# Flamingo block on one core: another queue order and opening for the first attention, another passage to the second, last weights split in 16 pieces

## The reference

```python
x = x + jnp.tanh(g_xattn[0]) * _L0_xattn_ref(_layernorm(x), ctx, fside, fside, Wq, Wkv, Wout, bout)
x = x + jnp.tanh(g_ffn[0])   * _L0_ffn_ref(_layernorm(x), router, gate_up, down, sh_gate, sh_up, sh_down, shared_gate)
x = x + jnp.tanh(g_xattn[1]) * _L1_xattn_ref(_layernorm(x), ctx, mask, Wq, Wk, Wv, Wo)
x = x + jnp.tanh(g_ffn[1])   * _L1_ffn_ref(x=_layernorm(x), Wg1, Wg2, Wup, bup, Wdown, bdown)
```

## Time and profile before

| | us |
|---|---|
| runs | 1830.37, 1835.76, 1840.65; median 1835.76 |
| the profiled execution, its own time | 1849.24 |
| its span (first to last instruction) | 1847.3 |
| PE busy | 1627.3 (88%) |
| VectorE (DVE) busy | 1158.1 (63%) |
| ACT busy | 733.5 (40%) |
| POOL busy | 411.9 (22%) |

### The profile page before, as it was taken

How to read it: one execution, slowest core, us unless ns; L and a number is a source line. 1 busy time by engine, 2 the same in 40 slices (tenths; PEclk the granted TensorE clock), 3 DMA queues, 4 the chain that set the end, 5 groups by cost and what they waited for, 6 DMA issues and landing times.

```text
span 1847.3 us, 42322 instructions
## 1 busy us (share of the span) xinstructions
PE 1627.3 (88%) x14740; PEld 1365.1 (74%) x14740; DVE 1158.1 (63%) x2986; ACT 733.5 (40%) x1494; POOL 411.9 (22%) x448
## 2 busy tenths in 40 slices
PE   2888988887798999999679999999999998699998
PEld 1555655555576778999678888888888887487887
DVE  4677777776566565555566666666666664465655
ACT  1555555553223223555333333333333332234443
POOL 2555555540323221000111212111121200000000
PEclk9899999999899999999889999999999998799999
DMA  7466566561101002543300000000000000000000
GB/s 190 100 118 117 117 117 117 117 115 33 46 31 39 23 27 79 175 128 114 126 21 21 20 28 20 26 20 26 20 23 26 23 11 7 5 12 23 11 23 23
DMA packets 127355, 107.06 MB, mean 58 GB/s; under 512 B 10442, under 2 KB 120195, under 8 KB 127020
## 3 DMA queue, kind: packets, MB, share of 16 engines
q1 hardware_dynamic: 121068, 89.07, 19.9%
q0 software_dynamic: 6208, 16.95, 2.9%
HBM read 49.22 MB, written 56.77 MB: 57 GB/s over the span
## 4 chain that ended last, share of the span: by engine, by line
PE 50%; DVE 24%; issue 12%; ACT 6%; DMA 3%; SPq 2%; DVEq 2%; another core or an unknown queue 1%; ACTq 0%; POOL 0%; POOLq 0%
PE bank L531 11%; PE bank L532 10%; PE bank L533 9%; PE bank L1006 3%; PE bank L602 2%; PE bank L1034 2%; PE bank L593 2%; DVE probs_b L2253 2%; DVE rm_b L2250 2%; PE bank L557 2%; DVE probs_a L1701 1%; DVE x L2154 1%; DVE oT_b_lo L2242 1%; PE bank L616 1%
## 5 line engine op out<-in xcount | busy, mean ns | idle before, releaser
L1567 POOL TENSOR_TENSOR probs_b<-probs_b,rs_b 128x512 f32<-128x512 f32 x64 | 66.7, 1043 | 483.1 <-DVE rs_b L2263 482.8
L531 PE MATMUL bank<-xT_b_hi,m_hi 128*128 128x256 f32 x512 | 153.7, 300 | 20.1 <-ACT qT L1376 12.0
L1397 ACT ACTIVATE probs_b<-probs_b 128x512 f32<-128x512 f32 x64 | 40.4, 632 | 324.1 <-DVE probs_b L2253 324.1
L531 PE MATMUL bank<-n_hi,oT_b_hi 128*128 128x256 f32 x512 | 149.8, 293 | 5.7 <-DVE x L2221 5.7
L532 PE MATMUL bank<-xT_b_hi,m_lo 128*128 128x256 f32 x512 | 145.7, 285 | 0.0
L533 PE MATMUL bank<-xT_b_lo,m_hi 128*128 128x256 f32 x512 | 145.6, 284 | 0.0
L532 PE MATMUL bank<-n_hi,oT_b_lo 128*128 128x256 f32 x512 | 145.2, 284 | 0.0
L533 PE MATMUL bank<-n_lo,oT_b_hi 128*128 128x256 f32 x512 | 145.1, 283 | 0.0
L1180 ACT ACTIVATE probs_a<-probs_a 128x512 f32<-128x512 f32 x128 | 80.3, 627 | 135.8 <-DVE probs_a L1701 135.2
L1006 PEld LDWEIGHTS bank<-ctxT_b,qT 128*128 128x128 f32 x1024 | 126.3, 194 | 2.7
L1006 PE MATMUL bank<-ctxT_b,qT 128*128 128x64 f32 x1024 | 122.7, 274 | 0.0
(11 more groups left out here) (316 smaller groups left out, 4919.3 us busy)
## 6 DMA issues: line engine op xcount, KB each, us to landing
sorted_x<-zeros SPq DMA_DIRECT2D x16, 2112.0 KB, 13.9
xg<-sorted_x SPq DMA_DIRECT2D x71, 128.0 KB, 2.1
sorted_y<-ys SPq DMA_DIRECT2D x71, 128.0 KB, 1.9
w_raw<-in_w SPq DMA_DIRECT2D x16, 408.0 KB, 4.0
x<-in_x SPq DMA_DIRECT2D x4, 1024.0 KB, 8.9
cx_raw<-in_ctx SPq DMA_DIRECT2D x32, 128.0 KB
out<-x SPq DMA_DIRECT2D x8, 512.0 KB, 2.9
ctxT_a<-in_ctxT SPq DMA_DIRECT2D x16, 128.0 KB, 2.1
```

The lines of the kernel that those rows point to most:

```text
L531: pe.matmul(dst, lh, rh, start=start, stop=False, skip_group_check=True)
L1567: pool.tensor_tensor(probs_b[b], probs_b[b], rs_b[:, b, :].unsqueeze(2).broadcast_to([P, G1, S]), ALU.mult).then_inc(s["b_probs"], 1)
```

## The change

- SP: only the first piece of `x` is loaded ahead of the tables; wv gets a semaphore of its own; pieces 1 to 3 of `x` come after wv; the rest of the tables is loaded in round 0, after the values of round 0.
- VectorE: statistics of piece 0 (8 tiles), 1/sd by integer guess and three Newton steps (`rsqrt`, L1640 on, in place of the root on ACT), keys(0), statistics of piece 1, queries(0), round 0. Pieces 2 and 3 are done inside round 0, the router weights are split after it. `queries(i+1)` moves from p = 1 to p = 2, ahead of `weigh0`.
- PE: transpose of x, both halves of the queries and values one slot later. ACT: `xT_copy` and `v_keep` one slot later. POOL: `queries_in` two slots later, the weights' low half one slot later; in the opening the masked keys before the queries.
- Passage: `w1_raw` is loaded after the first context of attention 1, so PE's `n` waits for `o1_raw` alone; VectorE does n_lo(0), tiles 0 and 1, n_lo(1), n_lo(2), statistics and norm, the other n_lo; PE's `turn_x1(0)` no longer waits for n_lo and `ones`. Tile 3 and the statistics of round 1 go into round 0, after `centre(0)`.
- `w1` is split in 16 pieces of 128x256, one in each round of the second attention: high half on ACT between `oth(i, 1)` and `pth(i, 2)`, low half on POOL at the round's end. The split on VectorE is gone.

```diff
             load_x(0)
-            load_x(1)
...
-                load_x(2 + n)
...
+            for n in range(1, 4):
+                load_x(n)
...
-            load_tables(slice(EARLY, NT * S), "tables_rest")
...
-            with sp.Fori(0, NA - 1) as i:
+            def next_round(i, rest=False):
                 sp.wait_ge(s["a_v_psum"], START + 1 + i)
                 load_context(i + 1)
+                if rest:
+                    load_tables(slice(EARLY, NT * S), "tables_rest")
                 load_round(i)
...
-            sp.dma_start(w1_raw, a["w1"]).then_inc(s["o1_loaded"], 16)
...
+            load_round1(0)
+            sp.dma_start(w1_raw, a["w1"]).then_inc(s["o1_loaded"], 16)
+            with sp.Fori(1, NA) as i:
+                load_round1(i)
...
                         if t == 0:
                             keys(i + 1)
-                        if t == 1:
+                        if t == 2:
                             turn_x(i + 1)
-                        if t in (2, 3):
-                            queries(i + 1, t - 2)
-                        if t == 5:
+                        if t in (3, 4):
+                            queries(i + 1, t - 3)
+                        if t == 6:
                             values(i + 1)
...
-            pe.wait_ge(s["o1_loaded"], 32)
+            pe.wait_ge(s["o1_loaded"], 16)
...
-            pe.wait_ge(s["mask_ready"], 2)
-            pe.wait_ge(s["n_copied"], H1 // 2)
-            pe.wait_ge(s["mask_ready"], 3)
...
             turn_x1(0, first=True)
+            pe.wait_ge(s["n_copied"], H1 // 2)
             for c in range(H1 // 2):
                 queries1(0, c)
+            pe.wait_ge(s["mask_ready"], 3)
...
                 oth(i, 1)
+                act.wait_ge(s["o1_loaded"], 32)
+                act.activation(w1_hi[:, ds(i * W1S, W1S)], w1_raw[:, ds(i * W1S, W1S)], ACT.Copy).then_inc(s["w0_hi"], 1)
                 pth(i, 2)
...
-                    if n == 4 and not last:
+                    if n == 6 and not last:
                         queries_in(i + 1, 0)
-                    if n == 5 and not last:
+                    if n == 7 and not last:
                         queries_in(i + 1, 1)
-                    if n == 6:
+                    if n == 7:
...
+                if first:
+                    pool.wait_ge(s["tables_rest"], 64)
...
+                pool.wait_ge(s["w0_hi"], START + NA + i + 1)
+                pool.tensor_tensor(w1_lo[:, i * W1S:i * W1S + W1S], w1_raw[:, i * W1S:i * W1S + W1S],
+                                   w1_hi[:, i * W1S:i * W1S + W1S], ALU.subtract).then_inc(s["w1_split"], 1)
...
-            stats(0)
+            def moments_x(n, at):
+
+                ve.wait_ge(s[f"x{n}_loaded"], 16)
+                for t in range(8):
+                    st.done(ve.bn_stats(bn[:, t, :], x[:, 8 * n + t, :]))
+                st.wait()
+                for t in range(8):
+                    st.done(ve.bn_aggr(mv_new[:, at + t, :], bn[:, t, :]))
+                st.wait()
+
+            moments_x(0, 0)
+            rsqrt(rstd[:, 0:8], nmr[:, 0:8], 8, 8)
             ve.sem_inc(s["stats_ready"], 1)
...
+                    if p == 2 and not last:
+                        queries(i + 1)
+                    if first and p < 2:
+                        moments_x(2 + p, 8 * p)
+                    if first and p == 1:
+                        rsqrt(rstd[:, 16:32], nmr[:, 16:32], 8, 16)
                     if p >= 2:
                         weigh0(i, p - 2)
...
-                    if p == 1 and not last:
-                        queries(i + 1)
...
             keys(0)
+            moments_x(1, 0)
+            rsqrt(rstd[:, 8:16], nmr[:, 8:16], 8, 8)
             queries(0)
-            ve.wait_ge(s["sel0_loaded"], 16)
+            attend0(0, first=True)
+            ve.wait_ge(s["w0x_loaded"], 160)
             st.done(ve.tensor_copy(rw0_hi, rw0_raw))
...
             ve.wait_ge(s["tables_rest"], 64)
-            attend0(0, first=True)
...
-            add_tile(0, more=1)
-            add_tile(1, yg1)
-            stats_b(0)
-            norm1(0)
             for c in range(H1 // 2):
...
+                if c == 0:
+                    add_tile(0, more=1)
+                    add_tile(1, yg1)
+                if c == 2:
+                    stats_b(0)
+                    norm1(0)
...
                 centre(0)
-                if not first:
+                if first:
+                    add_tile(3)
+                    stats_b(1)
+                else:
                     otl(i - 1, 3)
...
             add_tile(2)
-            add_tile(3)
-            stats_b(1)
-            ve.wait_ge(s["o1_loaded"], 32)
-            st.done(ve.tensor_copy(w1_hi, w1_raw))
-            st.wait()
-            ve.tensor_tensor(w1_lo, w1_raw, w1_hi, ALU.subtract).then_inc(s["w1_split"], 1)
```

More of the change, by code:

```diff
@@ L155, in build @@
         mv = keep.take("mean_var", NT, 2)
-        mv_new = keep.take("mean_var_new", 2 * FT, 2)
-        sd = keep.take("sd", NT)
+        mv_new = keep.take("mean_var_new", 4 * FT, 2)
+        sd = keep.take("sd", 56)
         rstd = keep.take("rstd", NT)
@@ L435, in load_round @@
                     "(p r c) -> p r c", p=P, c=CLEAR), zeros.unsqueeze(1).broadcast_to([P, REPEAT, CLEAR])).then_inc(s["rows_cleared"], 16)
-            with sp.Fori(0, NA - 1) as i:
+            def next_round(i, rest=False):
                 sp.wait_ge(s["a_v_psum"], START + 1 + i)
                 load_context(i + 1)
+                if rest:
+                    load_tables(slice(EARLY, NT * S), "tables_rest")
                 load_round(i)
+            next_round(0, rest=True)
+            with sp.Fori(1, NA - 1) as i:
+                next_round(i)
             load_round(NA - 1)
@@ L499, in _, with load_round1 @@
             sp.wait_ge(s["biases_stored"], 16)
-            with sp.Fori(0, NA) as i:
+            def load_round1(i):
                 sp.wait_ge(s["b_scores"], START + i * 4)
@@ L622, in outputs0, with project0 @@
                 m.then_inc(s["a_o_psum"], 1)
-            def project0(i, n):
+            def project0(i, n, first=False):
                 if n % 2 == 0:
@@ L630, in project0 @@
                     pe.wait_ge(s["a_resid"], START + i * 2 + p // 2)
+                if first and p == 0:
+                    pe.wait_ge(s["w0x_loaded"], 160)
                 m = pe.matmul(bank[5][:, 0:D], oT_a[:, p, :], wo0[:, p % 2, :], start=(p % 2 == 0), stop=(p % 2 == 1))
@@ L635, in late @@
             def late(i, t, lag, step, first):
-                if t >= lag:
+                if t >= lag and first and step is project0:
+                    step(i, t - lag, True)
+                elif t >= lag:
                     step(i, t - lag)
@@ L678, in _ @@
             queries(0, 1)
-            pe.wait_ge(s["w0x_loaded"], 208)
+            pe.wait_ge(s["wv_loaded"], 64)
             values(0)
@@ L1115, in root @@
                 act.wait_ge(s["sd_wanted"], n + 1)
-                act.activation(sd, sd, ACT.Sqrt).then_inc(s["sd_ready"], 1)
-            root(0)
+                act.activation(sd[:, 0:NT], sd[:, 0:NT], ACT.Sqrt).then_inc(s["sd_ready"], 1)
             NS = 8
@@ L1170, in attend0 @@
                 for t in range(NS + 5 if last else NS):
-                    if t == 6 and not last:
+                    if t == 7 and not last:
                         v_keep(i + 1)
@@ L1432, in _ @@
             oth(NA - 1, 3)
-            root(1)
+            root(0)
             ffn("f1", f1, NC1, HID1, False)
@@ L1515, in _ @@
             keys_in(0)
+            for n in range(AHEAD):
+                heads(0, n, first=True)
             queries_in(0, 0, first=True)
             queries_in(0, 1, first=True)
-            for n in range(AHEAD):
-                heads(0, n, first=True)
             bias(0)
-            pool.wait_ge(s["tables_rest"], 64)
             rounds(pool, NA, attend0)
@@ L1601, in _ @@
             ve.tensor_scalar(gbout, gbout, gates[:, 0:1], None, ALU.mult).then_inc(s["gbout_ready"], 1)
-            for n in range(4):
-                ve.wait_ge(s[f"x{n}_loaded"], 16)
-                for t in range(8 * n, 8 * n + 8):
-                    st.done(ve.bn_stats(bn[:, t % 8, :], x[:, t, :]))
-                st.wait()
-                for t in range(8 * n, 8 * n + 8):
-                    st.done(ve.bn_aggr(mv[:, t, :], bn[:, t % 8, :]))
-                st.wait()
             def moments(tile, count):
@@ L1625, in stats @@
             def stats(n):
-                ve.tensor_scalar(sd, mv[:, :, 1], LN_EPS, None, ALU.add).then_inc(s["sd_wanted"], 1)
+                ve.tensor_scalar(sd[:, 0:NT], mv[:, :, 1], LN_EPS, None, ALU.add).then_inc(s["sd_wanted"], 1)
                 ve.wait_ge(s["sd_ready"], n + 1)
-                st.done(ve.reciprocal(rstd, sd))
+                st.done(ve.reciprocal(rstd, sd[:, 0:NT]))
                 st.wait()
@@ L2321, in _ @@
             st.wait()
-            stats(1)
```

(1 more changed line is left out.)

15 lines of the change are left out of this document (8 added, 7 removed).

## The result

The kernel after takes 1815.13 us (median of 4 runs, 1813.28 to 1817.79), the kernel before beside it 1836.08 (4 runs, 1830.37 to 1840.65): ratio 0.9888, 95% interval 0.9861 to 0.9915, 21 us faster. The forecast was 1820. Measured again beside more runs of before the ratio was 0.9881 (0.986 to 0.9902). The kernel before took 1836 us here and 1850 to 1852 us beside the later kernels, so times are compared with those taken beside them, and otherwise only ratios are.

What follows compares the result with a forecast made beforehand. It took loads to bind the opening, a loop of engine hand-overs the first attention's rounds, weight loads and splits the passage, and PE the second attention. 7.2 + 2.1 + 6.4 = 15.7 us off 1835.8 gave 1820, range 1805 to 1834.

Steps and rivals of the forecast that it cites:

- Its sign: Whole kernel: faster, below 1826.6 us, with chance 0.76; same 0.18; slower, above 1844.9 us, 0.06.
- likeliest case: Whole kernel: the forecast itself, 1820 us, by itself 1811 to 1829; chance 0.57.
- Opening, forecast 7.2: Start of kernel: round 1 starts at 64.6 in place of 71.85, gaining 7.2 us, between 4 and 10.5.
- Rounds, forecast 2.1: First attention: a round falls from 23.57 to 23.4 us; 14 rounds x 0.15 = 2.1 us gained.
- The exchange at the centre of the count: First attention round: PE's queries come 2.41 us later, against VectorE's third pair of scores, 2.39 us, moved ahead of the rotary pair.
- a dip of the clock there costs as before: First attention rounds: two chains tie at 23.4 and 23.3 us, so a clock dip costs the same as before.
- Rival B: First attention: VectorE's wait was the bound, the loop falls towards PE's 20.78 us, 20 us more gained, 1800; chance 0.15.
- Passage, forecast 6.4: Passage to second attention: first queries 5.8 us earlier, second maximum at 926.3 against 932.66; 6.4 us gained, between 4 and 9.
- Pieces, forecast 0: Second attention: splitting the last weights in 16 pieces on ACT and POOL costs 0, at most 2 us on ACT.
- Rival D: First attention: PE drops to half clock in every round, 36 us slower, 1856; chance 0.08.

Runs made afterwards that it cites:

- b2_opening: Kernel after with PE, ACT and POOL rounds ordered as before, queries(0) ahead of piece 1's statistics, and one root for pieces 1 to 3: ratio to before 0.9761.
- r_all: Kernel before with only the new order of the first attention's rounds, on PE, ACT, POOL and VectorE: ratio 0.9935, 12 us faster.
- o_open: Kernel before with only the new opening; rounds, passage and last weights as before: ratio 0.996, 7 us faster.
- p_all: Kernel before with only the new passage and the last weights in 16 pieces; opening and first attention as before: ratio 0.995, 9 us faster.
- r_dve: Kernel before with one edit, VectorE's queries(i+1) at p = 2 ahead of weigh0; PE, ACT and POOL as before: ratio 0.9802, 37 us faster.
- b4_norder: b3_tile3 with VectorE's passage order as in before (tiles 0 and 1, statistics and norm ahead of all low halves): 1802.27 us, ratio to before 0.9738.
- b3_tile3: b2_opening with tile 3 and round 1's statistics put back ahead of the second attention's first maximum: 1801.42 us, ratio to before 0.9739.
- r_pe: Kernel before with only the new round order of PE, ACT and POOL; VectorE's queries(i+1) stay at p = 1: ratio 1.0324, 60 us slower.
- w4_pool: Kernel after with each of POOL's 16 subtractions for the last weights done four times: 1827.54 us against 1827.57 for the unchanged kernel after.

## Why the prediction was right, and where its sum was not

Its sign and its likeliest case hold, and 1815.13 is 5 us below 1820. The shares of the three parts don't: the rounds, which it gave least, gave most.

*Opening, forecast 7.2.* Found 6.2 in the profile (with the doubt on the clock of round 0 above), 7 by time. Every mark was 0.5 to 1.1 us late: the shuffle of the queries forecast for 30.6 came at 31.15, round 0 for 35.5 at 36.51, round 1 for 64.6 at 65.68. What it took for granted, that all statistics of piece 1 stand ahead of the first queries, was itself the cost that b2_opening took away.

*Rounds, forecast 2.1.* This is the term that was mis-sized: it measured 9.5 us from the start of round 1 to that of round 15, and r_all is 12 us faster by time. The exchange at the centre of the count is real, but it isn't even. The rotary pair starts 2.23 us later in the round (14.70 against 12.47), not 2.41; behind it VectorE's list is 2.73 us shorter (8.37 against 11.10), not 2.39 + 0.16. That makes 0.50 us a round in place of 0.15, or 13 times 0.50 = 6.4. The second miss was "a dip of the clock there costs as before": the three rounds at a clock of 0.93 are gone, which is another 4.3, and round 1 gives back 1.2 (25.18 against 23.99). Why the falls of the clock went away wasn't tested. But the three profiles with the old rounds (before, o_open, p_all) have two or three of them each, with stops of PE of 1.8 us in every round, and the kernels with shorter stops (1.3 us in after and r_all, 0.7 in r_dve, but for one in round 1) have none. Rival B, the wait as bound, was wrong for this change and right for one half of it: VectorE's move alone gives 21.68. The prediction had both halves' prices, 2.39 and 2.41, and netted them; the step it did not take was to ask whether the second was needed for the first.

*Passage, forecast 6.4.* Found 6.7: 7.1 up to the first queries (forecast 5.8) and -0.4 behind them (forecast 0.6). The new passage was well counted, 25.6 us from the first fold to the queries against a mean of 25.5; what was low is the old one, whose 31.38 is the least of five (mean 32.6). Of the 7.1, 3.5 come from VectorE's order, as b4_norder shows by taking it away, and the rest, by subtraction, from the fold that no longer waits for the other weights. Behind the queries two things cancel. Taking the split of 6.72 us off VectorE is worth 4.5 to 4.8 where tile 3 keeps its place (58.7 against 54.22 and 53.88 in b3_tile3 and b4_norder), and moving tile 3 behind the first maximum costs the 5 that b3_tile3 regains.

*Pieces, forecast 0.* Found 0, with four times the POOL work too.

*Rival D* didn't come: the clock in the rounds is 1.00. Its mechanism is real all the same: r_pe, the same order of PE, ACT and POOL without VectorE's move, runs at 0.88 in its longest rounds, and a round costs 4.4 us more than before, of which the longer wait explains 2.2. The Trainium skill (TensorE: Matmul & The Clock Gate, HAM oscillation) says that the clock falls after idle stretches; the trace of r_pe agrees with it, with one stop of 3.56 us and one fall in each round.

## What to carry to other kernels

When an edit moves work on several engines, price and run each half alone: here they were worth +37 and -60 us, and the pair 12, which is neither of them nor their sum. The wait on the path went away when other ready work of the same engine was put in front of it, and the awaited engine was then best left as it was. Filling a wait is worth only what must be done anyway behind it: look at what you put just behind the releaser, where tile 3 cost 5 us. And before a difference of two profiles is put down to an edit, compare a stretch that both kernels share: here it held 11 us of 31.

## What the runs showed of the hardware that was not expected

- In w4_pool, beside POOL's subtractions (both inputs in SBUF), VectorE's cast of one row, SBUF to SBUF, took about 654 ns in place of 271, in 15 of 16 rounds; its subtraction with an input in PSUM kept its 0.69 us beside the same POOL work. The Trainium skill (SBUF — State Buffer, Who interferes with whom) names casts among the VectorE operations that can contend with GpSimd for a shared pair of ports; this trace agrees. It cost some 6 us of VectorE in all (15 x 0.38) and none of the kernel's time.
- Feed-forward 0, equal in all kernels, took 426.6 us in one profile and 436 to 440 in the twelve others. In those twelve ACT stands once for 20 us, with PE idle for 12 of them, and is released by nothing that the profile names. Two profiles, compared as a whole, can be off by 10 us and more through this alone.
- In r_pe PE stopped for 3.56 us in each round, and the granted clock fell once in each; in rounds 1 to 14 of after, with stops of 1.3 us and one of 2.0, it didn't fall at all.
